# First attention rewritten as one list of slots, and the feed-forward's low-rank weight products computed in its last batch

## What is computed

```python
qkv = hidden_states @ w_qkv.T
q, k, v = jnp.split(qkv, 3, axis=-1)
q = _rms_norm(q, q_norm_w); k = _rms_norm(k, k_norm_w)
...
q = _rope(q); k = _rope(k)           # 16 heads of 16 numbers
mask = (q_idx >= k_idx) & (q_idx - k_idx <= WINDOW - 1)     # WINDOW 128
scores = jnp.einsum('bhqd,bhkd->bhqk', q, k) * scale
probs = jax.nn.softmax(jnp.where(mask, scores, -jnp.inf), axis=-1)
out = jnp.einsum('bhqk,bhkd->bhqd', probs, v)
return out @ w_o.T
...
w_up = dequant4bit(w_up_q, w_up_scale).T        # (q - 7.5) * scale
y1 = x1 @ w_up + b_up + x1 @ w_up_lora_a @ w_up_lora_b
x2 = jax.nn.relu(y1)
y2 = x2 @ w_down + b_down + x2 @ w_down_lora_a @ w_down_lora_b
```

## Time and profile before

| | us |
|---|---|
| median of 3 runs (1237.86 to 1242.57) | 1240.24 |
| the profiled execution | 1245.24 |
| its span in the profile | 1243.4 |
| busy in the span: PE / DVE / ACT / POOL | 1112.4 / 852.4 / 638.6 / 622.9 |
| first norm of the feed-forward begins at | 220.93 |
| first up product at | 252.60 |
| statistics of the scan's norm begin at | 307.79 |

### The profile page before, as it was taken

The page is one execution under the profiler, slowest core; times in us unless marked ns, Lnnn a source line. Parts: engine busy times, 40 slices in busy tenths (PEclk is TensorE's granted clock), DMA queues, the critical chain, the costliest instruction groups (busy, mean ns, idle before and its releaser), DMA issues. The chain is left out here.

```text
span 1243.4 us, 22588 instructions
## 1 busy us (share of the span) xinstructions
PE 1112.4 (89%) x6776; PEld 922.0 (74%) x6776; DVE 852.4 (69%) x2126; ACT 638.6 (51%) x2027; POOL 622.9 (50%) x648
## 2 busy tenths in 40 slices
PE   5499989688659966899999999999997999999998
PEld 4366656477425534899899989999996888888887
DVE  4767686553388886788878878888886455555555
ACT  4356644121359961666567656766672433443442
POOL 3633362253357763565456547644541545555554
PEclk9699988679769985999999999999996999999999
DMA  7000000000212402002000200000001111111111
GB/s 234 1 1 1 0 0 1 10 1 10 71 51 85 144 11 77 1 2 78 2 2 2 78 4 1 1 2 2 1 2 40 39 50 51 39 49 51 42 46 47
DMA packets 43967, 41.37 MB, mean 33 GB/s; under 512 B 6160, under 2 KB 39984, under 8 KB 43872
## 3 DMA queue, kind: packets, MB, share of 16 engines
q1 hardware_dynamic: 42144, 39.02, 10.1%
q10 hardware_dynamic: 1728, 1.18, 0.3%
HBM read 39.08 MB, written 1.11 MB: 32 GB/s over the span
## 5 line engine op out<-in xcount | busy, mean ns | idle before, releaser
L1732 POOL TENSOR_TENSOR hid_l<-hid,hid_h 128x512 fp32r<-128x512 f32 x66 | 85.5, 1296 | 132.5 <-ACT hid_h L1701 132.5
L1358 POOL TENSOR_TENSOR qr<-r_part_a,r_part_b 128x512 f32<-128x512 f32 x64 | 82.5, 1289 | 118.9 <-DVE r_part_b L1392 118.9
L1372 POOL TENSOR_TENSOR prob<-prob,rden 128x128 f32<-128x128 f32 (+1 forms) x256 | 123.8, 508 | 23.2 <-DVE rden L1443 22.6
L1782 DVE TENSOR_TENSOR hid<-psum,silu 128x512 f32<-128x512 f32 x66 | 45.6, 691 | 130.6 <-ACT silu L1699 130.6
L1318 ACT ACTIVATE prob<-psum,neg_max 128x128 f32<-128x128 f32 (+1 forms) x256 | 105.2, 418 | 41.1 <-DVE neg_max L1432 34.1
L1774 DVE SCALAR_TENSOR_TENSOR x<-psum,weight,x 128x256 f32<-128x256 f32 x264 | 108.8, 475 | 0.0
L73 PE MATMUL psum<-xt_h,gu_l 128*128 128x512 f32 x264 | 106.1, 402 | 2.4 <-POOL gu_l L1717 2.4
L75 PE MATMUL psum<-xt_h,gu_h 128*128 128x512 f32 x264 | 105.0, 398 | 0.0
L74 PE MATMUL psum<-xt_l,gu_h 128*128 128x512 f32 x264 | 104.5, 396 | 0.0
L1699 ACT ACTIVATE silu<-psum 128x512 f32<-128x512 f32 x66 | 39.5, 598 | 118.9 <-PE psum L75 118.9
L913 POOL TENSOR_TENSOR drive<-u,b_all 128x1024 f32<-128x1024 f32 x32 | 76.3, 2385 | 40.7 <-DVE h L1016 20.6
(11 more groups left out here) (251 smaller groups left out, 3752.1 us busy)
## 6 DMA issues: line engine op xcount, KB each, us to landing
b_all<-scan_b_rows SPq DMA_DIRECT2D x16, 512.0 KB, 3.6
early<-in_L_ffn_Wq_dram SPq DMA_DIRECT2D x4, 1024.0 KB, 5.3
early<-in_L_ffn_Wo_dram SPq DMA_DIRECT2D x4, 1024.0 KB, 8.1
raw<-in_L_ffn_Wg_dram SPq DMA_DIRECT2D x32, 128.0 KB, 2.2
raw<-in_L_ffn_Wu_dram SPq DMA_DIRECT2D x32, 128.0 KB, 2.3
raw<-in_L_ffn_Wd_dram SPq DMA_DIRECT2D x32, 128.0 KB, 2.2
x<-_attn_hidden_states_dram SPq DMA_DIRECT2D x8, 128.0 KB, 4.6
early<-in_L_ffn_w_up_q_dram SPq DMA_DIRECT2D x1, 1024.0 KB, 6.2
```

The costliest lines, as they stand in the source:

```text
L1358: pool.tensor_tensor(qr[:, i, :], part_a[:, slot, :], part_b[:, slot, :], ALU.add).then_inc(roped, 1)
L1372: ins = pool.tensor_tensor(at, at, rden[:, s % 4, i:i + 1].to_broadcast([P, (i + 1) * P]), ALU.mult)
L1732: pool.tensor_tensor(hid_l[:, j, cols], hid[:, c, :], f(hid_h[:, j, cols]), ALU.subtract)\
```

## The change

**The attention.** One function `schedule` now lists all kinds of work in one order, and each engine runs through it and does the kinds that it has. Only the first two tiles (batch 0) are projected, rotated and turned ahead; those of batch b + 1 are done between the heads of batch b, at fixed slots. Buffers hold two batches.

- q and k are stored as `stack`, high and low parts side by side, in four columns' groups per head (high, low, high, low for q; high, high, low, low for k), so that one transpose gives 64 rows per head, and one fp32r pass over 128 rows computes the scores of a pair of heads with all four cross products. k_t has zeros where the other head of the pair stands. This takes 16 transposes per tile.
- Scores are made for four heads in three units (`scores`): the first query tile of four heads, then the second one of two heads, twice. Each has a mask product of 512 columns.
- The probabilities are not divided. v has a column of ones, so that the value products (L679 to L681) also give the sums; the turned probabilities are now the stationary operand and 17 columns of v the moving one. `normalise` divides after eight heads.
- Copies of the turned probabilities go to ScalarE and VectorE in turns. The norm weights of q and k and the cosines are applied by VectorE straight from PSUM, and GpSimd scales by the inverse deviation afterwards.
- The attention output is turned (`turn_o`) and projected (`project_out`) in the following batch's slots.
- GpSimd clears k_t (8192 elements) behind the inverse deviations of the first norm, in place of clearing v (4096 elements) at the start; v (1088 elements) is now set to one there.

**The feed-forward.** Dequantizing is cut into 8 pieces in slots 12 to 19 (`dequantize`), the low-rank factors are loaded behind the weights on SP's queue, and their products are made in slots 2 to 9 of the last batch (`lora`). In `quantized_ffn`, VectorE subtracts for up's low part (`split_up`, L838) between ln_y and xt_l, and GpSimd does down's in four pieces (L827).

**The norms** share six semaphores with running counts; what they compute and in which order stays.

The diff, cut to its core:

```diff
+            for b in range(B):
+                t0, t1 = 2 * b + 2, 2 * b + 3
+                for slot in range(NH0):
+                    quad, hd = QUADS * b + slot // 4, slot % 4
+                    h = NH0 * b + slot
+                    ahead = hd < 3 and quad + 1 < QUADS * B
+                    if ahead:
+                        yield "scores", quad + 1, hd
+                    yield "turn", h
+                    if ahead:
+                        yield "peak", quad + 1, hd
+                        yield "exp", quad + 1, hd
+                    if h >= 1:
+                        yield "values", h - 1
+                        if h % GROUP == 0:
+                            yield "normalise", h // GROUP - 1
+                    if b >= 1 and slot == 1:
+                        yield "turn_o", b - 1
+                    if b >= 1 and slot == 8:
+                        yield "project_out", b - 1
+                    if b + 1 < B:
+                        if slot == 0:
+                            yield "qkv", t0
+                        if slot == 3:
+                            yield "qkv", t1
+                            yield "split", t0
+                        if 4 <= slot < 8:
+                            yield "turn_qk", t0, slot - 4
+                        if slot == 7:
+                            yield "split", t1
+                        if 9 <= slot < 12:
+                            yield "turn_qk", t1, slot - 9
+                        if slot == 11:
+                            yield "turn_qk", t1, 3
+                    if b == B - 1 and 2 <= slot < 2 + 2 * ffn.PIECES:
+                        yield "lora", slot - 2
+                    yield "dequantize", h
...
-                pool.memset(v[:], 0.0).then_inc(zeroed, 1)
+                pool.memset(v[:], 1.0).then_inc(zeroed, 1)
...
+                pool.memset(f(k_t[:]), 0.0).then_inc(zeroed, 1)
...
+                def qkv(t):
+                    cols = slice(2 * t, 2 * t + 2)
+                    pool.wait_ge(msq_ready, t + 1)
+                    pool.tensor_tensor(rqk[:, cols], msq[:, cols], core.neg_half[:, 0:2], ALU.pow).then_inc(rqk_ready, 1)
+                    pool.tensor_tensor(part_a[:], part_a[:], part_b[:], ALU.add).then_inc(rope_summed, 1)
+                    if t >= 1:
+                        pool.wait_ge(parts_lo, 2 * t)
+                    pool.wait_ge(rqk_ready, t + 1)
+                    pool.wait_ge(rope_summed, t + 1)
+                    pool.tensor_tensor(qr[:], part_a[:].rearrange("p (a n) -> p a n", a=2),
+                                       rqk[:, cols].rearrange("p (a n) -> p a n", n=1).to_broadcast([P, 2, D]), ALU.mult)\
+                        .then_inc(roped, 1)
...
+                def qkv(t):
+                    dve.wait_ge(squared, 2 * t + 2)
+                    if t >= 1:
+                        dve.wait_ge(roped, t)
+                    bank = psum[:, proj_bank("qk", t), :]
+                    dve.tensor_tensor(part_a[:], bank, cos_w[:, t % 2, :, :].rearrange("p a n -> p (a n)"), ALU.mult)
+                    xs, out = (a.rearrange("p (h c r) -> p h c r", c=2, r=HD0 // 2) for a in (bank, part_b[:]))
+                    sw = sin_w[:, t % 2, :, :].rearrange("p a (h c r) -> p (a h) c r", c=2, r=HD0 // 2)
+                    for c in range(2):
+                        ins = dve.tensor_tensor(out[:, :, c, :], xs[:, :, 1 - c, :], sw[:, :, c, :], ALU.mult)
+                    ins.then_inc(rope_done, 1)
+                    cols = slice(2 * t, 2 * t + 2)
+                    dve.tensor_scalar(msq[:, cols], sumsq[:, cols], 1.0 / D, 1e-6, ALU.mult, ALU.add).then_inc(msq_ready, 1)
+                def split(t):
                     for n in range(2):
+                        dve.wait_ge(parts_hi, 2 * t + n + 1)
+                        to, hi = (stack[:, 0, :, 1:4:2, :], stack[:, 0, :, 0:4:2, :]) if n == 0 else \
+                            (stack[:, 1, :, 2:4, :], stack[:, 1, :, 0:2, :])
+                        src = qr[:, n, :].rearrange("p (h a r) -> p h a r", h=NH0, a=1).to_broadcast([P, NH0, 2, HD0])
+                        dve.tensor_tensor(to, src, f(hi), ALU.subtract).then_inc(parts_lo, 1)
...
+                def turn(h):
+                    if h % 2 == 0:
+                        return
+                    dve.wait_ge(p_turned, h + 1)
+                    if h >= 4:
+                        dve.wait_ge(pv_done, h - 3)
+                    dve.tensor_copy(pt[:, h % 4, :], psum[:, PTURN[1], 0:W3]).then_inc(p_out[1], 1)
...
+                    if u == 0:
+                        for n in range(2):
+                            pe.matmul(bank[:, n * S:(n + 1) * S], q_t[:, b % 2, 2 * c + n, 0:P],
+                                      k_t[:, b % 2, 2 * c + n, :, 0:P], start=n == 0, stop=False, skip_group_check=True)
+                        masks = mask[:, 0:P].rearrange("p (a n) -> p a n", a=1).to_broadcast([P, 4, P])
+                    else:
+                        pair = 2 * c + u - 1
+                        pe.matmul(bank, q_t[:, b % 2, pair, P:S], k_t[:, b % 2, pair, :, :], start=True, stop=False,
+                                  skip_group_check=True)
+                        masks = mask[:, P:W3].rearrange("p (a n) -> p a n", a=1).to_broadcast([P, 2, S])
+                    pe.matmul(bank, core.ident_bf[:], masks, start=False, stop=True,
+                              skip_group_check=True).then_inc(scored, 1)
...
-                    pe.matmul(bank[:, 0:S], vs[:, par, 0, cols], pt[:, j % 2, 0:S], start=par == 0, stop=False,
-                              skip_group_check=True)
-                    ins = pe.matmul(bank[:, P:S], vs[:, par, 1, cols], pt[:, j % 2, S:], start=False, stop=par == 1,
...
+                    pe.matmul(out(0), part(0), keys(0), start=h % GROUP == 0, stop=False, skip_group_check=True)
+                    pe.matmul(out(1), part(1), keys(0), start=False, stop=False, skip_group_check=True)
+                    pe.matmul(out(1), part(2), keys(1), start=False, stop=h % GROUP == GROUP - 1, skip_group_check=True)\
+                        .then_inc(pv_done, 1)
...
-                act.wait_ge(weights, 1)
                 act.activation(up_h[:], up_s, ACT.Copy).then_inc(w_hi, 1)
                 norm.scalar(act)
-                act.wait_ge(weights, 2)
                 act.activation(down_h[:], down_s, ACT.Copy).then_inc(w_hi, 1)
                 act.wait_ge(loaded_b, 16 * 2)
                 for n in range(2 * KF):
...
             @block.gpsimd
             def _(pool):
                 norm.gpsimd(pool)
-                pool.wait_ge(w_hi, 1)
-                pool.tensor_tensor(up_l[:], up_s, f(up_h[:]), ALU.subtract).then_inc(w_lo, 1)
                 pool.wait_ge(w_hi, 2)
-                pool.tensor_tensor(down_l[:], down_s, f(down_h[:]), ALU.subtract).then_inc(w_lo, 1)
+                for k in range(0, KF, 2):
+                    rows = slice(k, k + 2)
+                    pool.tensor_tensor(down_l[:, rows, :], down_s[:, rows, :], f(down_h[:, rows, :]), ALU.subtract)\
+                        .then_inc(down_lo, 1)
...
-                def add_lora(n):
-                    raw = (up_s.rearrange("p k (c n) -> p (k c) n", c=UPC), down_s.rearrange("p (g k) n -> p g (k n)", g=4))[n]
-                    dve.wait_ge(ffn.scaled, n + 1)
-                    dve.wait_ge(lora_done, n + 1)
-                    dve.tensor_tensor(raw, psum[:, 4 * n:4 * n + 4, :], raw, ALU.add).then_inc(weights, 1)
-                norm.vector(dve, core.x, meanwhile=lambda: add_lora(0))
+                def split_up():
+                    dve.wait_ge(w_hi, 1)
+                    dve.tensor_tensor(up_l[:], up_s, f(up_h[:]), ALU.subtract).then_inc(up_lo, 1)
+                norm.vector(dve, core.x, between=split_up)
                 own = norm.count
-                add_lora(1)
...
-                ins.then_inc(lora_done, 1)
-                pe.wait_ge(weights, 1)
                 norm.tensor(pe)
-                for k in range(KF):
-                    ins = pe.matmul(psum[:, 4 + k // 2, (k % 2) * D:(k % 2 + 1) * D], lora_da[:, k * P:(k + 1) * P],
-                                    lora_db[:], start=True, stop=True)
-                ins.then_inc(lora_done, 1)
-                pe.wait_ge(weights, 2)
-                pe.wait_ge(w_lo, 1)
+                pe.wait_ge(up_lo, 1)
...
```

601 lines of the change are left out of this document (309 added, 292 removed).

## The result

| us | before | after |
|---|---|---|
| median of 20 runs each | 1242.03 | 1236.20 |
| lowest and highest run | 1237.86, 1245.04 | 1230.84, 1254.42 |
| the profiled execution / its span | 1245.24 / 1243.4 | 1232.23 / 1230.4 |
| first norm of the feed-forward | 220.93 | 228.70 |
| statistics of the scan's norm | 307.79 | 294.73 |

What follows compares the result with a forecast made beforehand. TensorE, never resting, was taken to bound the head loop and mostly to wait around it. Attention 14.3 us plus feed-forward 21.6 us gave 35.9 off 1240.24: 1204 us, range 1184 to 1229.

Steps and rivals of the forecast that it cites:

- Clock at the start 1.5: Head loop: 1.5 us lost to the clock at its start, one term of the 18.5 us that slots expose.
- the clock falls, and it is slower: Rival, head loop: stalls in every slot, TensorE granted 0.67, 65 us more plus idle share, 1270 us; chance 0.05.
- 18.5 in 150.9: Head loop: 18.5 us of exposed stalls and clock within 150.9 us of slots, far under 30%.
- Costs at full clock: Head loop, TensorE work at full clock: 1.45 us per head, 23.2 per batch, 132.4 in all.
- 3 for dequantizing: Slots 12 to 19: GpSimd's eight pieces, 20 us of work in some 18 us of slots, expose 3 us more.
- the four that I summed to 4 us per batch: Slots: stalls at qkv, next ScalarE copy, splits and the two-turn slot; 4 us per batch with tiles, 12 for three.
- Entry: Attention's start: clearing k_t blocks ln_y, input 5.8 us late at 26.3; first turn at 49.3 instead of 68.74.
- Tail: From the attention's last work to the feed-forward: as long as before, 6.4 us.
- Feed-forward: Feed-forward's start: first product 10.1 us after it instead of 31.7, 21.6 us won.

Runs made afterwards that it cites:

- A: The changed kernel itself, as the change left it, against the kernel before: median 1236.20 us, ratio 0.9955.
- C: A with k_t cleared early and one low-rank piece in every second slot of the last batch: median 1229.71 us, ratio 0.988.
- the two GpSimd variants: C with q and k low parts subtracted on GpSimd, 1259.36 us; the second also with values and normalising ahead of the peak every eighth head, 1270.99 us.

## Why the prediction was wrong

- **The clock.** The step that failed is "Clock at the start 1.5", and with it every term of the head loop, all priced at full clock: there was no term for a fall in the slots. I had a rival, *the clock falls, and it is slower*, at 0.05, and refuted it by the share of idle time (18.5 in 150.9). Two things in this were wrong. Stalls in every slot were not needed: the clock fell in one wait of 3.6 us, and the 27 us of nearly unbroken work behind it ran at 0.50. And beside the low-rank products it fell with no stall at all, and without them it stayed up to 215 us and the kernel took 1214.85. The earlier trace rows had such products at 0.50, busy for 7.19 of 7.30 us; I read that row as a price only, and did not ask whether the clock would be low beside them here too.
- **Its price.** First batch, from the first turn to the turn of its output: 41.0 in the run with the gap filled (45.27 to 86.29), 52.2 in A: 11.2. Last batch: 21.7 without the low-rank products, which at full clock cost 1.05 each in A (177.21 to 178.26), eight of them 8.4; 46.6 against 30.1 is 16.5 (against the 31.5 above, 15.1). Together 27.7 of the 35.9 us forecast.
- **Costs at full clock.** Right, and a little dear. With the clock up a batch with tiles takes 36.6 (82.33 to 118.97 with the gap filled) where I had 38, and 37.1 for the first (45.27 to 82.33) where I had 36 and 3 for dequantizing. Values take 0.59 per head where I had 0.68; only the low-rank products are dearer, 8.4 where I had 7.2. Of the stalls, the four that I summed to 4 us per batch are there (7.0 idle of 70 from 110 to 180), but one of them, in the first tile, is nearly as long as all four.
- **Entry.** The blocked ln_y came out as forecast (10.31 us for eight, 27.16 for the first product, 26.3 forecast), and clearing earlier showed it. The first turn came 3.3 late (52.63, forecast 49.3), 0.9 of it with the first product and the rest behind it.
- **Tail.** 6.85 from the last turn to the statistics at half clock and 6.84 in the run with six wide products beside each low-rank one (200.85 to 207.69): the clock was low in both by then. Forecast 6.4.
- **Feed-forward.** Right: first product 9.96 after its start (228.70 to 238.66, forecast 10.1), 20.8 us won (21.6).

The account closes: I had 1245.24 - 35.9 = 1209.3 for a profiled execution; the attention ended 22.1 late (228.70, forecast 206.6) and the feed-forward took 0.8 more: 1232.2, measured 1232.23. The 22.1 are 27.7 for the clock, 3.3 for the entry and 0.5 for the tail, less 9.4 by which slots at full clock (41.0 + 36.6 + 33.8 + 30.1 = 141.5) were cheaper than my 150.9. So the clock alone cost more than the error, and cheaper slots hid a part of it. The clock-free parts come from other kernels' traces, each of one execution.

## What to carry to other kernels

When a rewrite makes TensorE's products narrow or shallow, price it at both clocks, and look in the trace of before for work of the same shape at 0.50 while busy. The sum at full clock is not enough. Find the one longest wait in the new order, not only the sum of all waits: put wide products that are due anyway (a projection) into it or right behind it, and keep shallow ones apart. Useless wide products at such a place paid for themselves three times over in C (13.5 us of medians for 4) and once and a half in A (6 for 4).

## What the runs showed of the hardware

- A busy TensorE is not a fast one. 17-column fp32 products with 128-column transposes kept the row of 90 to 100 at 10.00 of 10 us busy, and the granted clock at 0.50. The Trainium skill ("TensorE: Matmul & The Clock Gate", "What's actually happening") has the clock follow how busy the engine has been; the trace disagrees as far as "busy" is read from its rows. The transposes are no smaller a part of the batches that ran at 1.00, and no run here separates them from the narrow products.
- During 32 products of 240 columns the clock rose to 1.00, 1.1 us behind their start in one trace and 3.0 in two others; during 3.9 us of 17-column products it did not. The 240-column ones were bf16, the others fp32.
- Beside products of 512 or 256 columns but 16 rows deep it fell from 1.00 to 0.50 without any idle time: in neighbouring slots at one of the first four, in every second slot anywhere from the first to the seventh, and with six wide ones beside each, in every second slot, at the sixth and the eighth. That depth is what matters there was not tested by itself.
- In the first two batches waits of TensorE of 3.6, 2.28 and 2.04 to 2.07 us each had a fall in them or within 1.1 us behind them, and so had three of about 1 us close together. One of 2.27 us in the third batch, behind an output projection, had none, and one fall (at 122) came 6.6 us behind a wait of 1.02. So no length of a wait alone tells it here.
- A GpSimd clearing of 7.02 us held up a VectorE tensor_scalar for 6.94 us where it takes 0.40.
- Open: whether the idle time or the narrow work around it brings the first fall; what decides, from run to run of one kernel, whether a later fall comes (12 to 24 us between runs; in the runs without low-rank products and with the early clearing, the profiled execution was the slowest, by 15 and 13 us over the next, and had a fall of 44 us in the second batch, but A's slower runs have no trace); and why the second of the two GpSimd variants was slower still.
